# Image 0's embedding placed first, one set of statistics for two layer norms, and stacking transfers per head

## What is computed

```python
h = patches @ Wp + bp + relu(xy @ W1 + b1) @ W2 + b2
a = layernorm(h)                            # eps 1e-5, no scale
n = (a - mean(a)) / sqrt(var(a) + 1e-5)     # the attention's own norm of a
q, k, v = split((n * ln_gamma + ln_beta) @ W_qkv.T)
gate = sigmoid(a @ W_gate.T + b_gate)
attn = softmax(q @ k.T * 32 ** -0.5)        # per head, 1024 x 1024
h = h + a + (einsum('bhij,bhid->bhjd', attn, v) * gate) @ W_final.T + b_final
z = layernorm(h)
H = gelu(z @ W1 + b1); probs = softmax(H @ Wg + bg)
h = h + probs[e] * (H @ Wd[e] + bd[e])      # e = argmax(probs)
```

## Time and profile before

| | |
|---|---|
| median of 3 runs | 1888.89 us (1886.69 to 1890.84) |
| the profiled execution | 1891.02 us, span 1889.2 us |
| PE busy | 1668.8 us, 88% |
| PEld busy | 1128.4 us, 60% |
| DVE busy | 1222.3 us, 65% |
| ACT busy | 946.8 us, 50% |
| POOL busy | 311.1 us, 16% |
| chain that ended last | PE 66%, DVE 19%, issue 7%, ACT 4%, DMA 1%, POOL 1% |

### The profile page before, as it was taken

The page is one execution under the profiler, slowest core; times in us unless marked ns, Lnnn a source line. Parts: engine busy times, 40 slices in busy tenths (PEclk is TensorE's granted clock), DMA queues, the critical chain, the costliest instruction groups (busy, mean ns, idle before and its releaser), DMA issues.

```text
span 1889.2 us, 29246 instructions
## 1 busy us (share of the span) xinstructions
PE 1668.8 (88%) x10884; PEld 1128.4 (60%) x10884; DVE 1222.3 (65%) x2027; ACT 946.8 (50%) x1564; POOL 311.1 (16%) x239
## 2 busy tenths in 40 slices
PE   8587799989999999999899999999797715999998
PEld 4445456646655564566466555645353504999998
DVE  0347767776776887677767768776766487444443
ACT  1144656575665657565746656475655330222222
POOL 0200200200020011002000200200000072455553
PEclk9789899999999999999999999999898957999999
DMA  3133041704342252417044432513060391566663
GB/s 117 34 92 95 15 106 51 156 1 116 96 101 62 79 129 46 107 51 156 4 121 100 91 83 65 129 38 90 11 146 1 85 205 62 181 202 206 205 198 133
DMA packets 124151, 187.31 MB, mean 99 GB/s; under 512 B 14941, under 2 KB 89325, under 8 KB 123888
## 3 DMA queue, kind: packets, MB, share of 16 engines
q1 hardware_dynamic: 108016, 121.48, 27.5%
q0 software_dynamic: 16000, 63.98, 10.4%
HBM read 84.72 MB, written 51.38 MB: 72 GB/s over the span
## 4 chain that ended last, share of the span: by engine, by line
PE 66%; DVE 19%; issue 7%; ACT 4%; DMA 1%; POOL 1%; SPq 1%; POOLq 0%; DVEq 0%; ACTq 0%
PE ps L481 12%; PE ps L722 11%; PE ps L495 10%; PE ps L448 8%; DVE nmax L1020 6%; PE ps L469 3%; PE ps L710 3%; DVE bst L873 3%; ACT pr L819 3%; PE ps L531 3%; PE ps L509 3%; PE ps L552 2%; PE ps L554 2%; PE ps L553 2%; PE ps L515 2%
## 5 line engine op out<-in xcount | busy, mean ns | idle before, releaser
L1020 DVE TENSOR_REDUCE nmax<-ps 128x1 f32<-128x1024 f32 x512 | 624.0, 1221 | 228.4 <-PE ps L481 219.5
L819 ACT ACTIVATE pr<-ps,nmax 128x1024 f32<-128x1024 f32 x512 | 570.1, 1114 | 302.5 <-DVE nmax L1020 297.6
L481 PE MATMUL ps<-stk,stq 96*128 96x512 f32 x1024 | 411.5, 486 | 78.2 <-ACT pr L819 57.9
L481 PEld LDWEIGHTS ps<-stk,stq 96*128 96x128 f32 x1024 | 171.6, 195 | 278.8 <-ACT pr L819 167.1
L495 PE MATMUL ps<-pr,vs 128*32 128x256 f32 x4096 | 275.1, 390 | 16.2 <-DVE vs L922 16.2
L722 PE MATMUL ps<-wd,hg 128*128 x1728 | 225.4, 287 | 0.0
L343 POOL TENSOR_SCALAR vare<-mv 128x8 f32<-128x8 f32 x24 | 5.7, 238 | 1311.2 <-DVE mv L877 1311.2
L722 PEld LDWEIGHTS ps<-wd,hg 128*128 128x128 f32 x1728 | 212.7, 193 | 0.0
L495 PEld LDWEIGHTS ps<-pr,vs 128*32 128x32 f32 x4096 | 109.8, 110 | 165.5 <-issue 78.5
L853 ACT ACTIVATE hg<-ps 128x512 fp32r<-128x512 f32 x144 | 78.5, 597 | 240.6 <-PE ps L710 240.6
L448 PE MATMUL ps<-wp,xt 128*128 128x256 f32 x768 | 196.1, 382 | 2.2 <-DMA xt<-x_in 1.5
(11 more groups left out here) (122 smaller groups left out, 1811.0 us busy)
## 6 DMA issues: line engine op xcount, KB each, us to landing
xt<-x_in SPq DMA_DIRECT2D x64, 384.0 KB, 3.1
stq<-qk SPq DMA_DIRECT2D x192, 128.0 KB, 2.5
stk<-qk SPq DMA_DIRECT2D x192, 128.0 KB, 2.5
token_rows<-staged_b SPq DMA_DIRECT2D x64, 256.0 KB, 4.2
token_rows<-staged_a SPq DMA_DIRECT2D x64, 256.0 KB, 4.5
token_rows<-hres POOLq DMA_DIRECT2D x8, 1024.0 KB, 5.2
wd_raw<-w_down SPq DMA_DIRECT2D x64, 128.0 KB, 3.3
rows<-token_rows,slot_from POOLq DMA_INDIRECT x72, 4.7
```

The lines of the kernel that those rows point to most:

```text
L481: last = mm(ps[:, 2 * (k % SR) + j, :], stq[:, hh, i * P:(i + 1) * P], stk[:, hh, j * 512:(j + 1) * 512], start=True, stop=True)
L819: actv(pr[:, k % PR, :], ps[:, 2 * (k % SR):2 * (k % SR) + 2, :].rearrange("p a n -> p (a n)"), ACT.Exp, bias=nmax[:, k % 16:k % 16 + 1], ...
L1020: V.reduce_max(nmax[:, k % 16:k % 16 + 1], ps[:, 2 * (k % SR):2 * (k % SR) + 2, :].rearrange("p a n -> p (a n)"), AX_X, negate=True).then_ ...
```

## The change

Start: SP issues two position loads, then all eight tiles of image 0 (tiles 2 to 7 into `x_first`, a part of `pr`), then seven early constants, then twelve others. The patch weights, the second position weights and the two bias rows (now copied to all partitions) are issued by ScalarE. TensorE embeds tiles 0 to 3, then alternates position terms of two tiles with one embedding (`position`, `first_embed`); the bias leaves the matmuls and is added by VectorE together with the position term. VectorE takes bn_stats of a tile while the next are made. The split of `wf1` follows the projections on ScalarE and VectorE, and its raw weights lie in `hres[:, 1]` instead of `a`. POOL waits for the constants before its first root.

Norms: since a = (h - m) / sqrt(v + eps) has mean 0 and variance v / (v + eps), n is (h - m) / sqrt((1 + eps) v + eps squared). So `stats_2` goes, POOL makes both roots in one power of twice the width, and n and a are both made from h, in this order, in `norm_2`.

Stacks: `stq` and `stk` become two halves of `st`. A transfer moves one stack of q and k of one head, 256 KB; 12 for a group. Each head has a semaphore, and each of the first four scores of a group waits for its own head.

```diff
-        stq = tensor(sa, "stq", [96, 4, TOKENS], F32R)
-        stk = tensor(sa, "stk", [96, 4, TOKENS], F32R)
+        st = tensor(sa, "st", [96, 2, 4, TOKENS], F32R)
+        stq, stk = st[:, 0], st[:, 1]
...
+        STACK = ((0, 3, 2), (1, 3, 1), (0, 4, 3))
...
+            for dst, src in ((posin, pos_in), (posw1, pos_w1)):
+                sp.dma_start(dst, src).then_inc(S["pos_in0"], 16)
+            for t in range(2):
+                sp.dma_start(xt[:, t], x[0, t]).then_inc(x_in[t], 16)
+            for t in range(2, TILES):
+                sp.dma_start(x_first[:, t - 2], x[0, t]).then_inc(S[f"x_first{t // 2 - 1}"], 16)
+            for dst, src in ((vecs[:, 0, :], ln_gamma), (vecs[:, 1, :], ln_beta), (vecs[:, 2, :], b_gate),
+                             (ident[:], identity), (wqk[:], w_qk), (wv[:], w_v), (wg[:], w_gate)):
+                sp.dma_start(dst, src).then_inc(S["early"], 16)
...
-                    for r in range(3):
-                        src = slice(32 * hh, 32 * hh + 32)
-                        dst = slice(32 * r, 32 * r + 32)
-                        sp.dma_start(stq[dst, hh, :].bitcast(F32), qk[src, 0, r % 2, :].bitcast(F32)
-                                     ).then_inc(stacked[g], 16)
-                        sp.dma_start(stk[dst, hh, :].bitcast(F32), qk[src, 1, r // 2, :].bitcast(F32)
-                                     ).then_inc(stacked[g], 16)
...
+                    src = slice(32 * hh, 32 * hh + 32)
+                    for r, (first, end, step) in enumerate(STACK):
+                        sp.dma_start(st[32 * r:32 * r + 32, :, hh, :].bitcast(F32),
+                                     qk_parts[src, first:end:step, :].bitcast(F32)).then_inc(stacked[g][hh], 16)
...
+            def root_1(b):
+
+                hold(pool, "var1", b + 1)
+                nc.gpsimd.tensor_scalar(vare[:, 0], mv[:, 0, :, 1], EPS, None, ALU.add).then_inc(S["eps1"], 1)
+                nc.gpsimd.tensor_scalar(vare[:, 1], mv[:, 0, :, 1], 1.0 + EPS, EPS * EPS, ALU.mult, ALU.add
+                                        ).then_inc(S["eps1"], 1)
+                wait(pool, "eps1", 2 * b + 2)
+                nc.gpsimd.tensor_tensor(rstd[:, 0:2], vare[:, 0:2], half_neg[:], ALU.pow).then_inc(S["rstd1"], 1)
...
+            pe.wait_ge(S["wp_in"], 16)
+            for t in range(4):
+                first_embed(t)
+            pe.wait_ge(S["pos_in1"], 16 * 2)
             pe.wait_ge(S["pos_relu"], 4)
...
+            for t in range(4):
+                position(2 * t)
+                position(2 * t + 1)
+                first_embed(t + 4)
...
-                wait(pe, "n_ready", b + 1)
+                wait(pe, ("n_ready", "a_ready")[w // 2], b + 1)
...
-                if k % G_STEPS == 0:
-                    wait(pe, stacked[g], (b * 24 + 24) * 16)
+                if k % G_STEPS < 4:
+                    wait(pe, stacked[g][hh], (b + 1) * 3 * 16)
...
+            nc.scalar.dma_start(wp[:], w_patch).then_inc(S["wp_in"], 16)
+            nc.scalar.dma_start(posw2, pos_w2).then_inc(S["pos_in1"], 16)
+            nc.scalar.dma_start(posbias, pos_bias[None, :, :].broadcast_to([P, 2, D])).then_inc(S["pos_in1"], 16)
...
+                    for hh in range(4):
+                        if g == 0:
+                            wait(act, stacked[1][hh], b * 3 * 16)
+                        else:
+                            wait(act, stacked[0][hh], (b + 1) * 3 * 16)
...
+            def norm_2(b, par, before):
                 if before:
                     wait(dve, "xt_mm", b * 4 - 4)
-                normalise(n, a, b, 2, "n_ready")
+                normalise(n, hres[:, par], b, 2, "n_ready")
+                normalise(a, hres[:, par], b, 1, "a_ready")
...
+                if t % 2 == 0:
+                    wait(dve, "pos_mm2", t + 2)
+                    V.tensor_tensor(posb[:, t:t + 2, :], ps[:, 4 + t // 2, :].rearrange("p (t d) -> p t d", t=2),
+                                    posbias[:, 0, None, :].broadcast_to([P, 2, D]), ALU.add).then_inc(S["pos_done"], 1)
...
-                        if after:
-                            stats_2(b + 1)
...
-                            norm_2(b + 1, before)
+                            norm_2(b + 1, 1 - par, before)
```

More of the change, by code:

```diff
@@ L190, in both @@
             return S[name + "0"], S[name + "1"]
-        x_in, stacked = both("x_in"), both("stack")
+        x_in = both("x_in")
+        stacked = [[S[f"stack{g}{hh}"] for hh in range(4)] for g in range(GROUPS)]
+        qk_parts = qk[:].rearrange("p w a t -> p (w a) t")
+        STACK = ((0, 3, 2), (1, 3, 1), (0, 4, 3))
         y_out = both("y_out")
@@ L251, in _ @@
         def _(sp):
[L252 to L259, removed]
+            for dst, src in ((posin, pos_in), (posw1, pos_w1)):
[7 more added lines that the diff above has]
+                sp.dma_start(dst, src).then_inc(S["early"], 16)
+            for dst, src in ((bfin[:], b_final), (wf1_in, w_ffn1), (wfin[:], w_final), (bf1[:], b_ffn1),
+                             (wr[:], w_router), (pick[:], pick_in), (up[:], upper), (rnk[:], rank), (brt[:], b_router),
+                             (sst[:], slot_start), (tid[:], token_id), (col[:], column)):
                 sp.dma_start(dst, src).then_inc(S["consts"], 16)
@@ L367, in image @@
                 if before:
-                    root(3, b - 1)
+                    root_3(b - 1)
                 if before:
@@ L374, in _ @@
             over_images(pool, image)
-            root(3, IMAGES - 1)
+            root_3(IMAGES - 1)
             store_rear(IMAGES - 1, (IMAGES - 1) % 2)
@@ L424, in spare, with position, first_embed @@
                 return ps[:, SPARE + j % 2, :]
-            pe.wait_ge(S["pos_in"], 16 * 4)
+            def position(t):
+                o = ps[:, 4 + t // 2, (t % 2) * D:(t % 2 + 1) * D]
+                for c in range(DC):
+                    last = mm(o, posr[:, c, t * P:(t + 1) * P], posw2[:, c, :], start=(c == 0), stop=(c == DC - 1),
+                              skip_group_check=True)
+                last.then_inc(S["pos_mm2"], 1)
+            def first_embed(t):
+                if t < 2:
+                    wait(pe, x_in[t], 16)
+                elif t % 2 == 0:
+                    wait(pe, f"x_first{t // 2 - 1}", 32)
+                source = xt[:, t] if t < 2 else x_first[:, t - 2]
+                for k in range(KC):
+                    last = mm(ps[:, t // 2, (t % 2) * D:(t % 2 + 1) * D], source[:, k, :], wp[:, k, :],
+                              start=(k == 0), stop=(k == KC - 1), skip_group_check=True)
+                last.then_inc(S["emb_mm"], 1)
@@ L591, in front_start @@
             def front_start(b):
-                for t in range(TILES):
-                    for part in range(3):
-                        embed(b, t, part)
-                wait(pe, "emb_h", b * TILES + TILES)
+                wait(pe, "pos_done", 4)
                 for j in range(8):
@@ L601, in front_start @@
                         project(b, 0, j, c)
+            pe.wait_ge(S["early"], 16 * N_EARLY)
+            front_start(0)
             pe.wait_ge(S["consts"], 16 * N_CONSTS)
-            front_start(0)
             def image(b, par, before, after):
@@ L874, in stats, with aggregate @@
                 last.then_inc(S[f"stats{ln}"], 1)
+                aggregate(b, ln)
+            def aggregate(b, ln):
                 hold(dve, f"stats{ln}", b + 1)
```

103 lines of the change are left out of this document (45 added, 58 removed).

## The result

The kernel after the change takes 1834.95 us (median of four runs, 1833.38 to 1835.67) against 1889.07 us for the one before in the same comparison: a ratio of 0.9713, with a 95% interval of 0.9696 to 0.9730. So the question is where some 9 us more than the sum came from.

The account below looks back on a forecast made before the run. Bound by a long chain of waits among TensorE, VectorE and ScalarE, no single engine. Gains 24.2 + 6.0 + 7.2 + 3.7 + 3.6 = 44.7 us took the profiled 1891.0 to 1846.3, less 2.1 for the median: 1844.2; range 1836 to 1857.

Parts of the forecast that it names:

- Part 1: Image 0's embedding: reordered loads and position terms bring the aggregates from 66.7 to 42.5, a gain of 24.2 us.
- the start is 3.5: TensorE's start: two small loads instead of four, the last issued about 0.7 us earlier, let it begin at 3.5 us.
- Rival C: Start: weights behind a table load and beside the tiles land late, near 15; 5 us lost, 1849; chance 0.06.
- B: Embedding of image 0: the clock stays at its lower level throughout; 25 us lost, 1869; chance 0.07.
- Part 2: Image 0's starting layer norms: one set of statistics, one wider power of 3.1 us; gain 6.0 us.
- Part 3: Image 0's first stacks: DMA engines limit 12 larger transfers; third exponential near 114.2 against 121.49, gain 7.2 us, elsewhere nothing.
- Rival D: Stacks: the three-level transfer pattern is expensive, making the kernel slower; 1915 at 2.4 us per transfer; chance 0.03.
- Rival A: Stacks: SP's issue was the limit, so scores run on without a pause; 1.4 us more gained, 1842.8; chance 0.08.
- Part 4: Middle of image 0: VectorE's shorter norm work brings the first maximum to 192.0 against 195.71; gain 3.7 us.
- Part 5: Router stretch of images 1 to 6: TensorE's 0.95 us wait for the logits copy goes; 0.6 each, 3.6 us.
- VectorE becomes last. Gain 0.4 to 0.8: Router stretch, images 1 to 6: VectorE's work, with `a` made after `n`, sets the end; 0.6 us taken per image.
- six such waits, one shown: Router, images 1 to 6: TensorE's 0.95 us wait for VectorE's logits copy, read in one image and counted for all six.

Follow-up runs that it names:

- loads_later: Kernel after, with the patch weights and image tiles issued only once the two small position loads have landed; 1834.57 us, ratio 0.9707.
- a_early: Kernel after, with the next image's `a` normalised between the two sets of four transposes ahead of the logits copy, not behind `n`; 1836.03 us, ratio 0.9729.
- norms_only: Kernel before, with only the one set of statistics for both layer norms, in all images; 1868.50 us, ratio 0.9901.
- a_early_dead: a_early plus eight unused statistics and eight unused aggregations at their old place in VectorE's queue; 1840.58 us, ratio 0.9731.
- before_delay: Kernel before, with one 128x2048 memset on VectorE ahead of image 0's statistics, delaying what follows; 1888.99 us, ratio 1.0003.
- start_only: Kernel before, with only the new order of image 0's tiles, loads and position term; 1865.99 us, ratio 0.9889.
- stacks_only: Kernel before, with only the stacking change: three transfers and one semaphore for each head; 1881.27 us, ratio 0.9964.
- two_rows: Kernel after without the third stack (q high times k low): eight transfers a group, scores over 64 rows; 1937.86 us, one execution.

## Why the prediction was right and wrong

**Part 1, mis-sized.** Forecast aggregates at 42.5, measured 45.06: a gain of 21.65 where 24.2 stood. The step that failed is "the start is 3.5": the small load took 4.05 us, not the 2.28 of the earlier trace rows, because large loads now stand right around it; loads_later, which holds them back, starts at 2.75. That is 1.8 us. The rest of the 2.5 is 0.2 in the position matmuls and 0.9 in the embedding, less 0.4 after it. The first pair took 7.67, more than the 4.15 + 2.6 of the sum. Rival C is out: the row at 12.42 has no idle before it. So is B: the last tile's row of twelve is done in 2.75 us, the rate of the later embeddings.

**Part 2, right.** Power 2.94 (forecast 3.1, between the bounds and near the upper one), aggregates to turn 6.63 (6.7), wait for `a` 0.55 (0.5). Gain 6.1 for 6.0.

**Part 3, right in kind.** From the first stacking issue, 18.2 us now pass to the third exponential, 25.0 before: 6.8 for 7.2. Twelve issues take 14.19 us, and both TensorE's fourth score and ScalarE's projection copy wait for head 3, as the text had it. The third score waits too, 0.64, which the sum had at nothing. Rival D is out, since the transfers go 1.26 us apart (median) and TensorE waits for a stack in image 0 alone. Rival A is out as well: the scores pause for 2.03 us, and with eight transfers they don't. The Trainium skill's 436 GB/s (DMA: Bandwidth & Descriptors, Anatomy of one DMA; there for DMAs that GpSimd issues) is not reached by these copies from SyncE: from 69 to 83 us the engines moved 188 GB/s at a busy share of 0.90.

**Part 4, right.** 4.07 for 3.7.

**Part 5, the step that failed.** Forecast 3.6, measured 212.77 - 201.36 = 11.4 over the six stretches. It fell apart in two places. First "VectorE becomes last. Gain 0.4 to 0.8": I added up VectorE's work from n's start to the last transpose and found 0.6. But from n's start to the end of the transposes VectorE now takes 11.33 us (315.96, the start of the eight normalisations into n, to 327.29), where I had 11.4 to 11.8 and 11.23 stood before: it is level with ScalarE's pace, not behind it, and a_early shows that there is nothing to save. And n starts 1.25 us earlier in the stretch, not 0.95 (22.30 us after the last maximum of the first group, 23.55 before); 0.12 of that is the waiting product itself, 0.95 us long against 1.06, and the rest I can't name. Less the 0.11 by which the maximum now follows n's start later, the term is 1.13 to 1.14, above its upper bound of 0.95, and 3.2 us more over six images. Second, a term that isn't in the sum at all: "six such waits, one shown" took image 1 for all. Three of the six stretches of the kernel before also held 3.4 us at half clock, 1.55 us each, 4.65 in all, and that too hangs on the removed wait. The Trainium skill (TensorE: Matmul & The Clock Gate, HAM oscillation — how this bites in real kernels) describes a kernel whose DMA waits of some 3 to 5 us each make the array start cold again. The trace has the low clock after a much shorter wait, 0.95 us, and not at its end but 1.0 to 2.4 us behind the start of the waiting product; I had looked for no such thing in this loop. The range's lower end let this part give 5.7 us at most, and so was 5.7 us short here.

**The sum again.** By the two repeats, which ran beside each other (1889.97 and 1835.82): to the end of the first 32 score steps 34.5, middle of image 0 4.1, routers 11.4, in small losses elsewhere -1.5, behind the last maximum 5.6, together 54.1. Against the forecast's 44.7: start and stacks -2.9, middle +0.4, routers +7.8, losses -1.5, end +5.6. The end was in no part of the forecast, and nothing shows it to be a merit of the change. In the two profiled executions of the kernel before and in norms_only, image 7's final products run partly at low clock, and the last of them starts 16.9 to 17.0 us after the last maximum (16.8 in a_early_dead); in before_delay, which has nothing of the change, in start_only and stacks_only, and in the kernel after and its repeat, 13.2. By these numbers the time lies below the range only with both: had either the routers given no more than the range allowed them, or the end nothing, it would have been near 1840.6, inside. The mechanism of part 5 was wrong whatever the end did; that the total fell outside took the end's luck as well. Kernel before, then kernel after (timeline, the first 32 of these products, which begin 8.1 and 6.4 us after that maximum):

```profile
1460.07 9.31 PE L531 MATMUL ps<-wfin,gate 128*128 128x256 f32 x32 [1.41 <-DVE gate L930]
```

```profile
1404.18 7.17 PE L558 MATMUL ps<-wfin,gate 128*128 128x256 f32 x32 [1.41 <-DVE gate L953]
```

A memset in front of image 0 was enough to take that away, yet it put a fourth slow stretch into the routers and 3.0 us into image 7's second group, and the time stayed (1.0003). What decides where these low stretches fall in a given program I can't say, and nor did any run here try to steer them. The profiled pair of the first comparison also has 3.4 us in image 7's first half, again low clock, which the repeat lacks.

Two sums on record are off by little: 9.2 + 2.6 from 0.95 earlier ends at 367.7, not 367.6, and the upper end adds up to 1856, not 1857. Neither bears on the outcome.

No kernel tried beats the kernel after by more than the measurement can tell.

## What to carry to other kernels

A wait repeated in a loop should be read in every turn of the loop, with the granted clock beside it: here the same 0.95 us wait cost 1.13 us in one image and 2.66 in the next. When work leaves one engine's queue, look at who waits behind it before adding up that engine's busy time: the gain was TensorE's, and it was larger than the wait. And when a small load is urgent, keep large ones from being issued right ahead of it or behind it, though what this gains can be lost again at the next place where the clock falls.

## What the runs showed of the hardware

A small load's landing depends on the large loads issued around it: 1.49 us with none, 4.05 for the same load with the patch weights 0.46 us ahead and the tiles 0.30 behind. (The 2.28 of the earlier trace rows is another load, the bias rows, with the patch weights 0.32 behind.)

A power over 16 columns takes 2.94 us on POOL where 8 take 1.67; by these two, an estimate is 0.16 a column and some 0.4 fixed.

Around score matmuls over 64 rows instead of 96 the weight loads start late. Timeline of two_rows, then the same embedding load in the kernel after, which has no idle:

```profile
100.55 0.29 PEld L508 LDWEIGHTS ps<-st 64*128 64x128 f32 x2 [0.33 <-issue]
...
101.21 0.73 PEld L475 LDWEIGHTS ps<-wp,xt 128*128 128x128 f32 x4 [0.36 <-issue]
```

```profile
100.51 0.86 PEld L475 LDWEIGHTS ps<-wp,xt 128*128 128x128 f32 x4
```

Over the whole kernel VectorE's maxima then wait longer for the scores, two_rows first:

```profile
L1054 DVE TENSOR_REDUCE nmax<-ps 128x1 f32<-128x1024 f32 x512 | 624.0, 1222 | 299.3 <-PE ps L508 294.9
```

```profile
L1054 DVE TENSOR_REDUCE nmax<-ps 128x1 f32<-128x1024 f32 x512 | 624.4, 1221 | 213.5 <-PE ps L508 204.8
```

These waits grow by 90 us, the kernel by 102. By the times from first to last maximum, the first groups of the eight images take 64 us more together and the second groups 27, of which some 15 are one low-clock stretch in image 5, from 1076.9 to 1111.1. The first group of image 7, where no embedding runs between the scores, also takes 11.2 more, so the embedding's loads alone aren't it. That the change of row count between neighbouring matmuls is the cause was argued from these rows and was not tried by itself.
